# GpSimd loads tokens behind the normalising, TensorE projects ahead of the first turn of a half, ScalarE squares ahead of copying that turn

## The chip, the cores and the metric

The kernel runs on one core of a Trainium2 chip. The metric is the device time of one execution in microseconds; before the change three runs gave a median of 3911.52 us. The engines have a queue each and meet only through semaphores: TensorE (PE), VectorE (DVE), ScalarE (ACT), GpSimd (POOL) and the queue that issues the DMAs (SP).

## What is computed

The input has 8 batches of 512 tokens of 128 features. A causal attention and a stack of six layers start from the normalised input, and both results are added to the input. The part that the change touches is the attention of a layer of the stack, with 16 heads of 64 and windows of 32 keys:

```python
for i in range(DEPTH):                                   # DEPTH = 6
    x = attn_layer(shift_tokens(x), Wqkv[i], q_scale[i], k_scale[i], Wo[i]) + x
    x = ffn_layer(shift_tokens(x), ln_g[i], ln_b[i], W1[i], b1[i], W2[i], b2[i]) + x

def attn_layer(x, Wqkv, qs, ksc, Wo):
    q, k, v = heads(x @ Wqkv)
    q = l2norm(q) * qs; k = l2norm(k) * ksc
    q = q * cos * scale + rotate_half(q) * sin * scale
    k = k * cos * inv + rotate_half(k) * sin * inv
    out = local_attention(q, k, v)                       # each query sees its window and the one before
    return out.transpose(0, 2, 1, 3).reshape(b, n, INNER) @ Wo
```

## The kernel before

All tokens of the stack stay in SBUF, transposed (xT). After the causal attention (about the first 490 us of the span) a loop runs over the six layers. In a layer the attention goes over 32 tiles of 128 tokens, tile by tile, and the feed-forward part follows.

**The pipeline.** Every engine runs the same function `pipeline(eng, step)`: one step a tile, six steps written out, a loop of six passes over four steps, and eight steps written out, which end with the draining. `behind(t, i, part, lag)` gives the tile that is `lag` steps back. In one step the engines work on several tiles: tile n is projected, n-1 is turned (transposed), n-2 is scored, n-3 is exponentiated, normalised and turned, n-3 or n-4 is weighed, n-5 or n-6 is projected out.

**The halves of a step.** A step has two halves, `wp` 0 and 1. The queries and keys of a tile come in four chunks of 512 columns (0 and 1 are the queries, 2 and 3 the keys); half `wp` handles chunks 2wp and 2wp+1. A chunk goes through these stations:

- `project(c)` on PE: three matmuls into bank pj[c % 2] (operands split in a high and a low part, one matmul short of all four). It waits for `sq` and `rotd`, that is, until the chunk two back has been squared and rotated. project(0) waits for `xs_ready` too, which GpSimd's `rests_of_tile` gives.
- `square(c)` on ACT (line 940), from the bank; then `rotate(c)` on DVE (line 1236), which waits for the square (`sq`) and for the `add` of the chunk two back (two buffers t12).
- `add(c)` on POOL (line 1505), which waits for `rotd` and for the turn of the same chunk of the tile before (`tr`).
- `scale(lag, c)` on POOL (line 1519), with `rn`, the inverse norms that ACT's `norms` makes (lines 949 to 956): chunks 0 and 1 in half 1 of the same step, chunks 2 and 3 in half 0 of the next.
- `turn_qk(c)` on PE (line 614): four transposes into rbank, when the chunk is scaled (`qn`) and when the chunk before it has been copied out of rbank (`ev`).
- `turned_qk(c)` on ACT (line 790): copies rbank out, in two copies for chunks 0 and 1, in one for 2 and 3.

Beside these run: `score(wp)` on PE with the mask that ACT's `mask_ahead` puts into the bank beforehand (it waits for `sub`, the subtraction of the maximum on DVE, line 1259); `exp` on ACT; `sums` on DVE; `normalise` on POOL (line 1527); `turn_p` on PE (line 645), which waits for the normalised half (`pn`); `windows()` on PE (line 673, in half 1), which transposes the tile's tokens into rbank and waits until chunk 2 has been copied out of it; `weigh` and `project_out`.

**Loading tokens.** POOL's `load_tile` copies the shifted tokens of the tile two ahead into `xs` in two instructions (lines 1475 and 1477), each of which waits for POOL's own one before it; before the change it runs in half 1 between add(2) and the scaling, and waits until add(2) has ended (`add`). ACT's `heads_of_tokens` and POOL's `rests_of_tile` (line 1484) split them.

The halves of the three engines before the change, in the order of their queues:

```
PE    turn_qk(2wp), project(2wp), project(2wp+1), turn_p, [windows], weigh, score, turn_qk(2wp+1), project_out
ACT   mask_ahead, turned_qk(2wp), square(2wp), square(2wp+1), exp, norms, [windows], turned_p, weighed, [heads], turned_qk(2wp+1)
POOL  add(2wp), [load_next], scale, scale, normalise, add(2wp+1), [rests_of_tile]
```

DVE's half is rotate(2wp), rotate(2wp+1), sums, the maximum and its subtraction, the sums of squares, and in half 0 of every other step the update of xT.

Of the kernel before, what the change touches and what calls it, by code (L numbers as in the profile page):

```python
# [92 lines left out]
def build(nc, ins, out, layers=DEPTH):  # L93
    ctx = ExitStack()
    with ctx:
# [55 lines left out]
        qn = take(4, 512)  # L151
# [97 lines left out]
        def behind(t, i, part, lag):  # L249

            s = t - lag
            if (part == 0 and s < 0) or (part == 2 and s >= 2 * TT):
                return None
            return s % TT, i + s // TT
# [144 lines left out]
        def _(pe):  # L399
# [153 lines left out]
            with pe.Fori(0, layers) as l:  # L553
# [14 lines left out]
                def step(t, i, part):  # L568
# [33 lines left out]
                    def turn_qk(c):  # L602
                        if not (v := behind(t, i, part, 1)):
                            return
                        tt, bt = v
                        g = g_of(bt) * 16 + (4 * tt + c)
                        pe.wait_ge(S["qn"], g + 7)

                        if c == 3:
                            pe.wait_ge(S["xwev"], g_of(bt) * 4 + tt + 1)  # L610
                        else:
                            pe.wait_ge(S["ev"], g)
                        for j in range(4):
                            m = nc.tensor.transpose(rbank[:, j * P:(j + 1) * P], qn[:, c, j * P:(j + 1) * P],  # L614
                                                    ident[:, :])
                        m.then_inc(S["tr"], 1)
# [77 lines left out]
                    if part == 2 and t == LAG + 2 * TT - 1:  # L694
# [5 lines left out]
                        for b in range(4):  # L700
                            mean(b)
                    for wp in range(2):
                        turn_qk(2 * wp)
                        project(2 * wp)
                        project(2 * wp + 1)
                        turn_p(wp)
                        if wp == 1:
                            windows()
                        weigh(4 - wp, 1 - wp)
                        score(wp)  # L710
                        turn_qk(2 * wp + 1)
                        project_out(wp)
# [75 lines left out]
        def _(act):  # L788
# [121 lines left out]
            with act.Fori(0, layers) as l:  # L910
# [11 lines left out]
                def step(t, i, part):  # L922
# [98 lines left out]

                    for wp in range(2):
                        mask_ahead(3 - wp, 1 - wp)
                        turned_qk(2 * wp)
                        square(2 * wp)
                        square(2 * wp + 1)
                        exp(3 - wp, 1 - wp)
                        norms(1 - wp, 1 - wp)
                        if wp == 1:
                            windows()  # L1030
                        turned_p(wp)
                        weighed(4 - wp, 1 - wp)
                        if wp == 0 and not (part == 0 and t == 0) and (v := behind(t, i, part, -1)):
                            heads_of_tokens(*v)
                        turned_qk(2 * wp + 1)
# [364 lines left out]
        def _(pool):  # L1400
# [63 lines left out]
            with pool.Fori(0, layers) as l:  # L1464
                def load_tile(tt, bt, again):

                    g = (l * B + bt) * 4 + tt
                    if again:
                        pool.wait_ge(S["proj"], g * 4 - 12)
                        pool.wait_ge(S["xwt"], g - 2)  # L1470
                    c0, base = WIN + tt * P, bt * T + tt * P
                    late = 1 if tt == 0 else 0
                    lower, upper = xs[0:64, c0:c0 + P], xs[64:128, c0 + late:c0 + P]
                    x_lower, x_upper = xT[0:64, bass.ds(base, P)], xT[64:128, bass.ds(base - 1 + late, P - late)]
                    pt_(lower, x_lower, xs[0:64, 0:1].to_broadcast([64, P]), ALU.subtract).then_inc(S["xs_lower"], 1)  # L1475
                    pool.wait_ge(S["xs_lower"], g + 1)
                    pt_(upper, x_upper, xs[64:128, 0:1].to_broadcast([64, P - late]), ALU.subtract).then_inc(S["xs_part"], 1)  # L1477
                    pool.wait_ge(S["xs_part"], g + 1)

                def rests_of_tile(tt, bt):  # L1480
                    g = (l * B + bt) * 4 + tt
                    c0 = WIN + tt * P
                    pool.wait_ge(S["xs_high"], g + 1)
                    pt_(xs_lo[:, tt, :], xs[:, c0:c0 + P], xs_hi[:, tt, :].bitcast(F32), ALU.subtract)\  # L1484
                        .then_inc(S["xs_ready"], 1)

                def step(t, i, part):
                    def g_of(bt):
                        return l * B + bt

                    def load_next():
                        if v := behind(t, i, part, -2):
                            tt, bt = v
                            pool.wait_ge(S["add"], (g_of(bt) * 4 + tt) * 4 - 4)
                            load_tile(*v, not (part == 0 and t + 2 < TT))

                    def add(c):
                        if not (v := behind(t, i, part, 0)):
                            return
                        tt, bt = v  # L1500
                        g = g_of(bt) * 16 + (4 * tt + c)
                        pool.wait_ge(S["tr"], g)
                        pool.wait_ge(S["rotd"], g + 2)
                        swapped = t12[:, c % 2, 1, :].rearrange("p (h e d) -> p h e d", h=8, e=2)[:, :, ::-1, :]
                        pt_(qn[:, c, :].rearrange("p (h e d) -> p h e d", h=8, e=2),  # L1505
                            t12[:, c % 2, 0, :].rearrange("p (h e d) -> p h e d", h=8, e=2), swapped, ALU.add)\
                            .then_inc(S["add"], 1)

                    def scale(lag, c):
                        if not (v := behind(t, i, part, lag)):  # L1510
                            return
                        tt, bt = v
                        g = g_of(bt) * 16 + (4 * tt + c)
                        half = c // 2
                        pool.wait_ge(S["rn"], g_of(bt) * 8 + (2 * tt + half + 1))
                        pool.wait_ge(S["add"], g + 2)
                        r = rn[:, tt % 2, half, 8 * (c % 2):8 * (c % 2) + 8].unsqueeze(2).to_broadcast([P, 8, D])
                        sums_of_heads = qn[:, c, :].rearrange("p (h d) -> p h d", h=8)
                        pt_(sums_of_heads, sums_of_heads, r, ALU.mult).then_inc(S["qn"], 1)  # L1519

                    def normalise(lag, wp):
                        if not (v := behind(t, i, part, lag)):
                            return
                        tt, bt = v
                        m_ = g_of(bt) * 8 + 2 * tt + wp
                        pool.wait_ge(S["srec"], m_ + 1)
                        pt_(dd[:, wp, :].rearrange("p (h k) -> p h k", h=HP),  # L1527
                            dd[:, wp, :].rearrange("p (h k) -> p h k", h=HP),
                            srec[:, wp, :].unsqueeze(2).to_broadcast([P, HP, 64]), ALU.mult).then_inc(S["pn"], 1)

                    for wp in range(2):
                        add(2 * wp)
                        if wp == 1:
                            load_next()
                        scale(1 - wp, 2 - 2 * wp)
                        scale(1 - wp, 3 - 2 * wp)
                        normalise(3 - wp, 1 - wp)
                        add(2 * wp + 1)
                        if wp == 0 and not (part == 0 and t == 0) and (v := behind(t, i, part, -1)):
                            rests_of_tile(*v)  # L1540

                pool.wait_ge(S["mx"], l * B)
                pool.wait_ge(S["kT_zero"], 1)
                pool.wait_ge(S["ul"], l * (3 * B))
                load_tile(0, 0, False)
                rests_of_tile(0, 0)
                load_tile(1, 0, False)
                rests_of_tile(1, 0)
                pipeline(pool, step)

                with pool.Fori(0, B // 2) as j:
                    for e in range(2):
                        n = l * B + 2 * j + e
                        for c, (f0, fn) in enumerate(FCH):
                            pool.wait_ge(S["uh"], n * 3 + c + 1)
                            pt_(uu_lo[e][c][0:fn], uu[0:fn, e, c, :], uu_hi[e][c][0:fn].bitcast(F32), ALU.subtract)\
                                .then_inc(S["ul"], 1)
# [47 lines left out]
```

## Time and profile before

| | |
|---|---|
| median of 3 runs | 3911.52 us (3907.31 to 3912.17) |
| the profiled execution: its own time, its span | 3916.98 us, 3915.2 us |
| PE busy (matmuls) | 3617.0 us, 92% |
| PE busy (weight loads) | 2685.2 us, 69% |
| ACT busy | 3010.4 us, 77% |
| DVE busy | 2778.3 us, 71% |
| POOL busy | 2730.6 us, 70% |
| granted TensorE clock, mean | 0.96 |
| DMA | 5.8% of 16 engines' span |

Busy times are unions of an engine's instructions. Matmuls are pipelined and their ends are modelled, so that one matmul's row reaches into the next one's; what a matmul occupies is read from the distance between starts. In a row of the order in time, the time in brackets is how long the engine had been idle and who ended it; gaps under 0.15 us are not shown there and have to be read from the starts.

### The profile page before, as it was taken

To read this page: it belongs to the slowest core of one execution; us is meant where nothing else is said; L and a number is where in the kernel's file an instruction comes from. 1 tells how busy PE (TensorE), PEld (TensorE's weight loads), DVE (VectorE), ACT (ScalarE), POOL (GpSimd) and SP (SyncE) were. 2 spreads that over 40 slices of the span, in tenths; PEclk is the share of its full clock that TensorE was granted. 3 is DMA by queue.
4 is the path that set the end of the run, shared out by engine and by line. 5 is a ranking of instruction groups with operands and counts; after the bars stand their busy time and mean duration, and the time that the engine had idled before them with its cause. 6 is when DMAs were issued, how large, how long until landed. Compare 5 with 4: busy or idle time off the path is not lost.

```text
span 3915.2 us, 94663 instructions
## 1 busy us (share of the span) xinstructions
PE 3617.0 (92%) x30894; PEld 2685.2 (69%) x30894; DVE 2778.3 (71%) x3770; ACT 3010.4 (77%) x6096; POOL 2730.6 (70%) x2889
## 2 busy tenths in 40 slices
PE   6898689999889999899999899999799999799998
PEld 3444367777667777677777677777577776577776
DVE  4566377776677776677776677776677776677776
ACT  3555478888688887688887688886688886788885
POOL 3454378886388884588884688883688882788872
PEclk7999789999999999899999899999899999899999
DMA  4223200000100000000001000001000001000002
GB/s 132 85 90 92 56 1 1 0 0 1 30 2 1 0 0 22 9 2 0 0 0 29 2 2 0 0 0 29 2 2 0 0 0 29 2 1 0 0 1 71
DMA packets 59745, 67.76 MB, mean 17 GB/s; under 512 B 12006, under 2 KB 40164, under 8 KB 58468
## 3 DMA queue, kind: packets, MB, share of 16 engines
q1 hardware_dynamic: 59492, 64.64, 5.8%
q8 instruction: 128, 2.10, 0.2%
q14 instruction: 125, 1.02, 0.1%
HBM read 46.27 MB, written 18.35 MB: 17 GB/s over the span
## 4 chain that ended last, share of the span: by engine, by line
POOL 41%; issue 29%; PE 19%; ACT 5%; DVE 3%; POOLq 2%; DMA 1%; SPq 1%; ACTq 0%; DVEq 0%
PE bank L401 16%; POOL sb_area L1505 16%; POOL sb_area L1519 12%; POOL sb_area L1527 6%; POOL sb_xs L1477 2%; POOL sb_xs L1475 2%; POOL sb_xwin L1484 2%; PE bank L614 2%; ACT sb_area L790 1%; DVE sb_area L1157 1%; ACT sb_area L940 1%; ACT sb_area L983 1%; DMA sb_wqk_lo<-qk_rows 1%; ACT sb_area L842 0%; ACT sb_lnb L952 0%
## 5 line engine op out<-in xcount | busy, mean ns | idle before, releaser
L790 ACT ACTIVATE sb_area<-bank 128x512 f32<-128x512 f32 (+4 forms) x2149 | 1315.2, 648 | 266.2 <-PE bank L614 206.4
L1236 DVE TENSOR_TENSOR sb_area<-bank,sb_rots 128x1024 f32<-128x1024 f32 x768 | 907.4, 1220 | 625.6 <-ACT sb_area L940 619.0
L1505 POOL TENSOR_TENSOR sb_area<-sb_area 128x512 f32<-128x512 f32 x768 | 983.6, 1281 | 311.8 <-DVE sb_area L1236 311.3
L401 PE MATMUL bank<-sb_area 128*64 128x64 f32 (+6 forms) x17104 | 1053.9, 276 | 10.2 <-DMA sb_area<-in_c_crot 3.5
L401 PEld LDWEIGHTS bank<-sb_area 128*64 128x64 f32 (+4 forms) x17104 | 750.0, 146 | 280.8 <-issue 244.0
L1519 POOL TENSOR_TENSOR sb_area<-sb_area,sb_rn 128x512 f32<-128x512 f32 x768 | 785.0, 1043 | 49.9 <-POOL sb_xs L1477 40.8
L401 PE MATMUL bank<-sb_area,sb_wvo 128*128 128x256 f32 x3072 | 728.3, 381 | 3.1 <-DVE sb_xT L1291 3.1
L401 PE MATMUL bank<-sb_wqk_hi,sb_xwin 128*128 128x512 f32 x1536 | 606.6, 436 | 43.0 <-POOL sb_xwin L1484 38.4
L614 PE MATMUL bank<-sb_ident,sb_area 128*128 128x128 f32 x3072 | 507.3, 288 | 134.1 <-POOL sb_area L1519 90.0
L401 PEld LDWEIGHTS bank<-sb_area,sb_wvo 128*128 128x128 f32 x3072 | 555.0, 190 | 75.2 <-issue 8.8
L614 PEld LDWEIGHTS bank<-sb_ident,sb_area 128*128 128x128 f32 x3072 | 330.9, 143 | 304.4 <-POOL sb_area L1519 211.7
L940 ACT ACTIVATE sb_area<-bank 128x512 f32<-128x512 f32 x768 | 439.2, 597 | 82.8 <-PE bank L401 42.7
L1246 DVE TENSOR_REDUCE sb_ssq<-sb_area 128x16 f32<-128x1024 f32 x384 | 464.1, 1209 | 0.0
L1527 POOL TENSOR_TENSOR sb_area<-sb_area,sb_srec 128x512 f32<-128x512 f32 x384 | 401.2, 1045 | 81.1 <-DVE sb_srec L1271 81.1
L401 PE MATMUL bank<-sb_wqk_lo,sb_xwin 128*128 128x512 f32 (+4 forms) x1280 | 423.0, 414 | 29.7 <-POOL sb_xwin L1412 13.8
L401 PEld LDWEIGHTS bank<-sb_wqk_hi,sb_xwin 128*128 128x128 f32 x1536 | 303.3, 197 | 109.0 <-issue 43.4
L790 ACT ACTIVATE bank<-sb_lmask 128x512 f32<-128x512 bf16 x384 | 231.0, 601 | 100.7 <-DVE sb_area L1259 95.1
L1269 DVE TENSOR_REDUCE sb_ssum<-sb_area 128x8 f32<-128x512 f32 x384 | 260.0, 677 | 45.6 <-ACT sb_area L983 45.6
L1259 DVE TENSOR_TENSOR sb_area<-bank,sb_smax 128x512 f32<-128x512 f32 x384 | 265.6, 692 | 13.1
L1256 DVE TENSOR_REDUCE sb_smax<-bank 128x8 f32<-128x512 f32 x384 | 253.0, 659 | 24.8 <-PE bank L401 24.5
L401 PEld LDWEIGHTS bank<-sb_wqk_lo,sb_xwin 128*128 128x128 f32 (+1 forms) x1280 | 206.4, 200 | 88.5 <-issue 26.8
L1157 DVE TENSOR_REDUCE sb_area<-bank 128x2 f32<-128x1024 f32 (+3 forms) x256 | 203.6, 823 | 88.6 <-PE bank L401 87.1
(116 smaller groups left out, 4107.3 us busy)
## 6 DMA issues: line engine op xcount, KB each, us to landing
qk_rows<-sb_p SPq DMA_DIRECT2D x52, 256.0 KB, 4.2
sb_wqk_hi<-qk_rows SPq DMA_DIRECT2D x32, 256.0 KB, 2.9
sb_wqk_lo<-qk_rows SPq DMA_DIRECT2D x32, 256.0 KB, 2.7
sb_area<-in_Wqkv SPq DMA_DIRECT2D x7, 1024.0 KB, 5.7
sb_area<-in_WvT SPq DMA_DIRECT2D x7, 512.0 KB, 7.5
sb_wo_bd<-in_Wo SPq DMA_DIRECT2D x14, 256.0 KB, 8.5
sb_area<-in_x SPq DMA_DIRECT2D x4, 512.0 KB, 6.0
sb_area<-in_x SPq DMA_DIRECT2D x8, 256.0 KB, 2.9
```

The costliest lines, as they stand in the source:

```text
L401: return nc.tensor.matmul(o, a, b, start=start, stop=stop, skip_group_check=True)
L614: m = nc.tensor.transpose(rbank[:, j * P:(j + 1) * P], qn[:, c, j * P:(j + 1) * P], ident[:, :])
L790: return nc.scalar.activation(o, i, ACT.Copy)
L940: nc.scalar.activation(sqb[:, c, :], pj[c % 2][:, :], ACT.Square).then_inc(S["sq"], 1)
L1236: tt_(t12[:, c % 2, :, :].rearrange("p u (h d) -> p u h d", h=8), src, bc(rots[:, tt, s, :, :], [P, 2, 8, D], 2), ALU.mult).then_inc(S["ro ...
L1246: nc.vector.tensor_reduce(ssq[:, tt % 2, half, :], sqb[:, 2 * half:2 * half + 2, :].rearrange("p c (h d) -> p (c h) d", h=8), AX.X, ALU.add)\
L1256: nc.vector.tensor_reduce(smax[:, wp, :], s3, AX.X, ALU.max).then_inc(S["smax"], 1)
L1259: tt_(dd[:, wp, :].rearrange("p (h k) -> p h k", h=HP), s3, bc(smax[:, wp, :], [P, HP, 64], 2), ALU.subtract).then_inc(S["sub"], 1)
L1269: nc.vector.tensor_reduce(ssum[:, wp, :], d3, AX.X, ALU.add).then_inc(S["ssum"], 1)
L1505: pt_(qn[:, c, :].rearrange("p (h e d) -> p h e d", h=8, e=2), t12[:, c % 2, 0, :].rearrange("p (h e d) -> p h e d", h=8, e=2), swapped, A ...
L1519: pt_(sums_of_heads, sums_of_heads, r, ALU.mult).then_inc(S["qn"], 1)
L1527: pt_(dd[:, wp, :].rearrange("p (h k) -> p h k", h=HP), dd[:, wp, :].rearrange("p (h k) -> p h k", h=HP), srec[:, wp, :].unsqueeze(2).to_b ...
```

## The change

Three edits of the order within a half.

- PE: `project(2wp)` comes before `turn_qk(2wp)` instead of behind it; `project(2wp+1)` still follows.
- ACT: `square(2wp)` comes before `turned_qk(2wp)`.
- POOL: `load_next()` stands behind `normalise` and ahead of `add(2wp+1)` in half 1. Its wait for add(2) is replaced by waits for the scaling of chunks 0 and 1 of this tile and for the normalising just before it.

```diff
@@ PE
                     for wp in range(2):
+                        project(2 * wp)
                         turn_qk(2 * wp)
-                        project(2 * wp)
                         project(2 * wp + 1)
@@ ACT
                         mask_ahead(3 - wp, 1 - wp)
+                        square(2 * wp)
                         turned_qk(2 * wp)
-                        square(2 * wp)
                         square(2 * wp + 1)
@@ POOL
                         if v := behind(t, i, part, -2):
                             tt, bt = v
-                            pool.wait_ge(S["add"], (g_of(bt) * 4 + tt) * 4 - 4)
+                            pool.wait_ge(S["qn"], (g_of(bt) * 4 + tt) * 4)
+                            if last := behind(t, i, part, 2):
+                                pool.wait_ge(S["pn"], g_of(last[1]) * 8 + 2 * last[0] + 2)
                             load_tile(*v, not (part == 0 and t + 2 < TT))
@@
                         add(2 * wp)
-                        if wp == 1:
-                            load_next()
                         scale(1 - wp, 2 - 2 * wp)
                         scale(1 - wp, 3 - 2 * wp)
                         normalise(3 - wp, 1 - wp)
+                        if wp == 1:
+                            load_next()
                         add(2 * wp + 1)
```

## Rows read from the trace of the kernel before

**Rows 1.** The page's chain of work that ended last, by engine.

```profile
POOL 41%; issue 29%; PE 19%; ACT 5%; DVE 3%; POOLq 2%; DMA 1%; SPq 1%; ACTq 0%; DVEq 0%
```

**Rows 2.** Busy time by stretch: engines, then granted clock, DMA share, GB/s.

```profile
1632.00:1700.00 68.00, 52.43 (x430) 39.68 (x430) 47.91 (x53) 49.51 (x109) 54.91 (x58) 0.84 0.00 1
1700.00:2060.00 360.00, 353.84 (x3312) 274.36 (x3310) 279.56 (x362) 314.48 (x647) 306.37 (x325) 1.00 0.00 0
```

**Rows 3.** POOL in order of time: first add of a layer's first and last tile.

```profile
1632.05 2.65 POOL L1505 TENSOR_TENSOR sb_area<-sb_area 128x512 f32<-128x512 f32 x2 [2.17 <-DVE sb_area L1236]
...
2074.62 1.28 POOL L1505 TENSOR_TENSOR sb_area<-sb_area 128x512 f32<-128x512 f32 x1 [1.95 <-DVE sb_area L1236]
```

**Rows 4.** PE in order of time, one tile: half 1 from 2020.42, half 0 from 2027.63.

```profile
2020.42 0.63 PE L614 MATMUL bank<-sb_ident,sb_area 128*128 128x128 f32 x4
2020.81 0.48 PE L401 MATMUL bank<-sb_wqk_hi,sb_xwin 128*128 128x512 f32 x1
2021.13 0.40 PE L401 MATMUL bank<-sb_wqk_lo,sb_xwin 128*128 128x512 f32 x1
...
2022.30 0.60 PE L645 MATMUL bank<-sb_ident,sb_area 128*128 128x128 f32 x4
2022.73 0.38 PE L673 MATMUL bank<-sb_ident,sb_xs 128*128 128x128 f32 x2
2023.05 2.22 PE L401 MATMUL bank<-sb_area 64*128 64x256 f32 x40
...
2025.69 1.89 PE L401 MATMUL bank<-sb_area,sb_wvo 128*128 128x256 f32 x8
2027.63 0.66 PE L614 MATMUL bank<-sb_ident,sb_area 128*128 128x128 f32 x4
...
2029.63 0.66 PE L645 MATMUL bank<-sb_ident,sb_area 128*128 128x128 f32 x4
2030.22 2.22 PE L401 MATMUL bank<-sb_area 64*128 64x256 f32 x40
...
2032.86 1.89 PE L401 MATMUL bank<-sb_area,sb_wvo 128*128 128x256 f32 x8
2034.81 0.63 PE L614 MATMUL bank<-sb_ident,sb_area 128*128 128x128 f32 x4
```

**Rows 5.** POOL in order of time, from add(2) to the next tile's add(0).

```profile
2023.73 1.28 POOL L1505 TENSOR_TENSOR sb_area<-sb_area 128x512 f32<-128x512 f32 x1 [0.69 <-DVE sb_area L1236]
2025.34 0.39 POOL L1475 TENSOR_TENSOR sb_xs<-sb_xT,sb_xs 64x128 f32<-64x128 f32 x1 [0.33 <-POOL sb_area L1505]
...
2026.53 2.04 POOL L1519 TENSOR_TENSOR sb_area<-sb_area,sb_rn 128x512 f32<-128x512 f32 x2 [0.23 <-POOL sb_xs L1477]
2028.54 1.04 POOL L1527 TENSOR_TENSOR sb_area<-sb_area,sb_srec 128x512 f32<-128x512 f32 x1
...
2031.48 1.27 POOL L1505 TENSOR_TENSOR sb_area<-sb_area 128x512 f32<-128x512 f32 x1 [0.67 <-DVE sb_area L1236]
```

**Rows 6.** ACT in order of time, half 0.

```profile
2028.32 1.20 ACT L790 ACTIVATE sb_area<-bank 64x512 f32<-64x512 f32 x2 [0.79 <-PE bank L614]
2029.55 1.08 ACT L940 ACTIVATE sb_area<-bank 128x512 f32<-128x512 f32 x2
...
2031.71 0.22 ACT L956 ACTIVATE sb_rn<-sb_lnb 128x16 f32<-128x16 f32 x1
...
2033.48 1.18 ACT L790 ACTIVATE sb_area<-bank 64x512 f32<-64x512 f32 x2
2034.68 0.60 ACT L790 ACTIVATE bank<-sb_lmask 128x512 f32<-128x512 bf16 x1
```

**Rows 7.** DVE in order of time, half 0: the two rotations, the subtraction.

```profile
2030.18 2.36 DVE L1236 TENSOR_TENSOR sb_area<-bank,sb_rots 128x1024 f32<-128x1024 f32 x2 [2.16 <-ACT sb_area L940]
...
2033.95 0.69 DVE L1259 TENSOR_TENSOR sb_area<-bank,sb_smax 128x512 f32<-128x512 f32 x1
```

**Rows 8.** PE in order of time, turn of the second tile of a layer.

```profile
1639.25 0.80 PE L614 MATMUL bank<-sb_ident,sb_area 128*128 128x128 f32 x4 [2.66 <-POOL sb_area L1519]
```

## The prediction

> **What bounds the kernel now.** I looked first at how the time is shared between stages. From the first add of a layer's first tile to the first add of its last one 2074.62 - 1632.05 = 442.6 us pass [rows 3], six times over; the rest of a layer (the draining, the feed-forward part) and the causal part ahead of the layers hold none of the edited steps' steady running. I then read the busy time by stretch [rows 2]. In the 360 us in the middle of a layer the granted clock is 1.00, the upper level of 2.4 GHz, and PE is busy for 353.84 us, while ACT, POOL and DVE have 314, 306 and 280. In the first 68 us of a layer PE has only 52.43 and the clock is 0.84: there PE waits.
>
> That row says "PE is full", the chain of what ended last says "POOL 41%, PE 19%" [rows 1]. The order in time settles it, because a matmul's row reaches into the next one's. I compare equal steps of PE in the two halves of one tile [rows 4]:
>
> - The eight matmuls of `project_out` show 1.89 us, of which 0.38 is the last one's own length; seven starts in 1.51 make 0.216 each, 1.73 for eight. The next turn starts 1.94 us (2025.69 to 2027.63) and 1.95 us (2032.86 to 2034.81) after the first of them. So PE stands idle for 0.21 and 0.22 us ahead of each `turn_qk(2wp)`.
> - Turn and projections take 1.88 us in half 1 (2020.42 to 2022.30) and 2.00 in half 0 (2027.63 to 2029.63): 0.12 idle ahead of turn_p(0).
> - turn_p and the hand-over to weighing take 0.59 in half 0 (2029.63 to 2030.22). In half 1 the four transposes take 0.43, and the windows' two, which end with the same hand-over, take 0.32 where two alone would take 0.22: 0.43 + 0.10 = 0.53. That is 0.06 more.
>
> Together 0.61 us of a tile's 14.39 (2020.42 to 2034.81); PE's own work is 13.78 us a tile. Who ends these waits: the scaling of chunk 0 ends at about 2027.57, halfway in a row of two that starts at 2026.53, and turn_qk(0) starts at 2027.63; the normalising ends at 2029.58, and turn_p(0) starts at 2029.63 [rows 4, 5]. Before turn_qk(2) it is ACT's copy of chunk 1, which ends at 2034.66 [rows 4, 6].
>
> So one round closes a tile, and it goes through all engines: normalise, turn_p(0), weigh, score, turn_qk(1), project_out, turn_qk(2), its copy, square(2), rotate(2), add(2), **the load**, the two scalings, normalise. The load stands in it with 2026.53 - 2023.73 = 2.80 less an add of 1.28, 1.52 us [rows 5]. A second round through turn_qk(0), its two copies, square(0) and rotate(0) explains why add(0) waits for 0.67 us [rows 5 to 7].
>
> **The change, part by part.** I lay the new order out from the start of project(0), call that moment 0, and look for what is late next.
>
> *GpSimd.* Nothing is added but a wait. add(2) to the end of add(3) held 7.09 us of unbroken work (2023.73 to 2030.82: the normalising starts at 2028.54 and takes 1.00 to the next start, the add 1.28) [rows 5], and still does, since the load only changes its place. Scalings and normalising come 1.52 us earlier. The two waits of PE on them were 0.21 and about 0.18 us long, so both vanish, with over 1.1 us to spare. The load now waits for the normalising instead of for add(2): the same kind of wait for its own engine, 0.33 before the first and 0.23 behind the second instruction [rows 5], cost 0. What is behind it in the queue is add(3), at the same distance from add(2) as before.
>
> *TensorE.* project(0) no longer stands behind turn_qk, and waits for squares and rotations two chunks back, which are over half a step old. turn_qk(2wp) comes 0.79 later: the copy of chunk 1, 0.19 late before, is now in time. The price: six projection matmuls in one go take 1.49 us (2020.81 to 2022.30), the first 0.32 (to 2021.13), so the others 0.234 each [rows 4]. Now each group of three may begin with a slow start: at most 0.32 - 0.23 = 0.09 a half, 0.18 a tile; at least 0, since the trace has no projection directly behind a project_out. I take the middle, 0.09: PE's work is 13.87, between 13.78 and 13.96.
>
> *ScalarE.* The first chunk is ready 0.32 + 0.23 + 0.40 + about 0.04 = 0.99 after its projection starts. In the old half 0, ACT runs without a visible gap from 2028.32 to 2035.28 (the mask's 2034.68 + 0.60), 6.96 us [rows 6]; the new order holds the same pieces. So square(2) starts at 7.95, ends at 8.55 (two squares in 1.08, one some 0.60), and the copy of chunk 2 (about 0.61) ends at 9.16. PE waits for that copy before `windows`: project(0) to project(2) takes 6.83 (old half 0 is 7.18, less the waits of 0.22, 0.12 and 0.06, plus half of the 0.09 for this half; at most 0.05 more), then 1.94 for the two projections around the turn and 0.43 for turn_p: 9.20. With a crossing of 0.04 to 0.15 (2034.66 to 2034.81 is 0.15) PE waits for 0 to 0.11 there. I add 0.03. DVE's rotate(2) follows square(2) at once, before the copy, which is what the edit is for.
>
> A tile then takes **13.90 us instead of 14.39, 0.49 less**, between 13.78 and 14.07.
>
> *How many tiles.* 26 of the 31 distances in a layer at 14.39 make 374 us, and leave 68 for the five of the filling, 13.7 each. So 6 x 26 = 156 tiles gain 0.49: 76 us. In the filling PE waits much longer, 2.66 us in one place, for the same scaling [rows 8], and its busy time is 52 of 68 us [rows 2]: there the round is the bound, and the edits take from it the load (1.52) and the copies ahead of the squares (1.20 and 0.60). Part of this runs into PE's own work and into the half-speed clock, so I bound it by 0 and 2 us a tile and take 1: 6 x 5 x 1 = 30 us. The draining, I hold, is unchanged.
>
> **Sum.** 3917.0 us (the profiled execution's own time, span 3915.2) - 76 - 30 = 3811. The median of the runs shown, 3911.5, lies 5.5 lower, so I forecast 3806.
>
> **A rule against the row on busy time.** Read as it stands, the row of the middle stretch leaves 360 - 353.84, or 1.7%, 0.25 us a tile, to be gained at most [rows 2]; the starts leave 0.61. By the first the edits can bring 156 x 0.25 = 38 us and no more, 3874. The Trainium skill (Perfetto Trace Analysis, Identifying the Most-Contended Engine) says that the busy share of matmuls is no good measure of how near TensorE is to its limit, and wants the weight loads looked at. By that rule there is more room than 1.7%; the trace agrees in that weight loads are busy for 274.36 of the 360 us, 76%.
>
> **Rivals.**
>
> 1. *PE is as full as its busy time says.* For it: 98% busy, clock at its upper level. Against it: the unequal lengths of equal steps in [rows 4]. Time: 3874. Chance 0.07.
> 2. *ScalarE takes over the wait.* Its copy of chunk 2 is due within 0.1 us by my sum. If ACT's half gets 0.3 us longer (square and copy no longer overlap as two squares do, or the mask waits), PE waits for it at `windows`: 14.20 a tile, nothing in the filling; 156 x 0.19 = 30 us, 3882. For it: ACT has no gap in that half. Against: 0.6 us between the subtraction's end (2034.64) and the mask in the new order. Chance 0.06.
> 3. *Slower: the load in front of add(3).* add(3) frees the buffer that rotate(1) of the next tile writes. add(2) starts at 6.83 + 2.92 (0.99 + 0.60 + 0.03 + 1.22 + 0.08) = 9.75, and add(3) ends 7.09 later, at 16.84, which is 2.94 in the next tile. rotate(1) wants to start behind square(1), at 3.43, and the subtraction ends 3.3 after that start (2030.18 plus half of the pair's 2.36 is about 2031.3; 2033.95 + 0.69 is 2034.64 [rows 7]), at 6.75; the mask is due at 7.35. So there are 0.5 + 0.6 = 1.1 us of slack; beyond it each us of delay is one in the tile, through mask, square(2), rotate(2), add(2). It decides against the change when the load's way is more than 1.6 us longer than now, twice its length. With 2.1 us, 14.90 a tile: 156 x 0.51 = 80 us more, 3991. For it: GpSimd has 7.09 us of work in a half of 7.04. Against: nothing in the load changes. Chance 0.07.
> 4. *No change.* Another round of 14.39 us stands behind the one removed, one that I have not seen. The distances above show none. 3911. Chance 0.05.
>
> **How the numbers follow.** My forecast has 0.75. Its own range is 156 x (0.32 to 0.61) = 50 to 95 us and 0 to 60 in the filling: 3756 to 3862. About 2% of a tile either way covers the rest; reaching to the first rival's time, without rivals 2 to 4, gives 3755 to 3875, which leaves out about 0.2. Changes under 0.2% (8 us) cannot be told from none here. Faster: 0.75 + 0.07 + 0.06 = 0.88; same 0.05; slower 0.07.
>
> **What would show it.** In the changed profile, starts of turn_qk(0) one tile apart are 13.9 us apart (13.8 to 14.05). No idle time in brackets before L614 by POOL L1519 in the middle of a layer; if one is left on PE it is before L673, by ACT L790. The load's 0.33 follows L1527. POOL's wait for DVE before add(0) is gone or shorter, and a wait of some 0.5 us for ACT's L956 appears before the scaling in half 0, since rn, 3.61 after the first copy's start [rows 6], is ready at 4.6 and add(0) is over at 4.2; it costs nothing, as turn_qk(2) is due at 7.6. The first five tiles of a layer take 62 to 64 us instead of 68. I am wrong if a tile stays over 14.1, if the idle time of PE moves to L673 with more than 0.15 us, or if the matmuls behind project_out start at more than 0.32.

## The result: 3754.85 us, 4% less

The changed kernel takes 3754.85 us (median of 4 runs, 3744.81 to 3760.0) where the kernel before takes 3911.85 in the same comparison. The ratio is 0.9596, with a 95% interval of 0.9572 to 0.962: 157 us less. The forecast was 3806, with a range from 3755 to 3875. The direction was right, and so was the round of waits that the change was to open. But the gain was half as large again as predicted (157 us for 105), one of the three edits was credited with what the other two do, and the time lies 0.15 us outside the range.

The profiled execution took 3744.81 us, its span is 3743.1. Its chain of work that ended last, by engine, answers to [rows 1]:

```profile
PE 75%; issue 11%; ACT 5%; DVE 3%; POOL 3%; DMA 1%; SPq 1%; ACTq 0%; POOLq 0%; DVEq 0%
```

It was POOL with 41% and is PE with 75%. The busy time by stretch of the third layer, its filling and its middle (the columns are those of [rows 2]):

```profile
1568.80:1632.00 63.20, 50.37 (x442) 37.78 (x443) 51.16 (x58) 51.53 (x114) 58.19 (x62) 0.91 0.01 1
1632.00:1980.00 348.00, 347.95 (x3408) 285.58 (x3407) 290.93 (x370) 313.54 (x661) 312.18 (x330) 1.00 0.00 0
```

In the middle the busy rows of PE leave no idle time, and its weight loads are busy for 82% (76% before). In the filling the granted clock is 0.91 where it was 0.84. The first add of that layer's first and last tile, in GpSimd's order of time, answers to [rows 3]:

```profile
1568.81 2.65 POOL L1507 TENSOR_TENSOR sb_area<-sb_area 128x512 f32<-128x512 f32 x2 [2.16 <-DVE sb_area L1236]
...
1983.57 1.28 POOL L1507 TENSOR_TENSOR sb_area<-sb_area 128x512 f32<-128x512 f32 x1 [1.25 <-DVE sb_area L1236]
```

That is 414.8 us instead of 442.6. PE's order of time for one tile, half 1 from 1863.79 and half 0 from 1870.81, with the project_out ahead of it, answers to [rows 4]:

```profile
1862.25 1.89 PE L401 MATMUL bank<-sb_area,sb_wvo 128*128 128x256 f32 x8
1863.79 0.58 PE L401 MATMUL bank<-sb_wqk_hi,sb_xwin 128*128 128x512 f32 x1
1864.20 0.40 PE L401 MATMUL bank<-sb_wqk_lo,sb_xwin 128*128 128x512 f32 x1
...
1864.67 0.65 PE L614 MATMUL bank<-sb_ident,sb_area 128*128 128x128 f32 x4
1865.08 0.48 PE L401 MATMUL bank<-sb_wqk_hi,sb_xwin 128*128 128x512 f32 x1
...
1865.87 0.60 PE L645 MATMUL bank<-sb_ident,sb_area 128*128 128x128 f32 x4
1866.31 0.39 PE L673 MATMUL bank<-sb_ident,sb_xs 128*128 128x128 f32 x2
...
1869.27 1.89 PE L401 MATMUL bank<-sb_area,sb_wvo 128*128 128x256 f32 x8
1870.81 0.59 PE L401 MATMUL bank<-sb_wqk_hi,sb_xwin 128*128 128x512 f32 x1
...
1871.71 0.60 PE L614 MATMUL bank<-sb_ident,sb_area 128*128 128x128 f32 x4
1872.06 0.48 PE L401 MATMUL bank<-sb_wqk_hi,sb_xwin 128*128 128x512 f32 x1
...
1872.84 0.60 PE L645 MATMUL bank<-sb_ident,sb_area 128*128 128x128 f32 x4
...
1877.55 0.58 PE L401 MATMUL bank<-sb_wqk_hi,sb_xwin 128*128 128x512 f32 x1
```

No row has a bracket. A tile is 13.76 us long here (1863.79 to 1877.55) and 13.69 as a median. From the first matmul of project_out to turn_p it is 3.57 us in half 0 (1869.27 to 1872.84), and 3.62 in this half 1 (1862.25 to 1865.87), where the turn takes 0.41 us to the next start instead of 0.35. The parts of the kernel before were 1.73 + 1.88 = 3.61 by the prediction's reading, and its turn in there took 0.39 (2020.42 to 2020.81); with a turn of 0.35 they are 3.57 too. So the new order costs PE nothing.

GpSimd from add(2) to the next add(0), as in [rows 5], but in the new order:

```profile
1908.05 1.28 POOL L1507 TENSOR_TENSOR sb_area<-sb_area 128x512 f32<-128x512 f32 x1 [0.39 <-DVE sb_area L1236]
1909.28 2.05 POOL L1521 TENSOR_TENSOR sb_area<-sb_area,sb_rn 128x512 f32<-128x512 f32 x2
1911.28 1.05 POOL L1529 TENSOR_TENSOR sb_area<-sb_area,sb_srec 128x512 f32<-128x512 f32 x1
1912.71 0.39 POOL L1475 TENSOR_TENSOR sb_xs<-sb_xT,sb_xs 64x128 f32<-64x128 f32 x1 [0.38 <-POOL sb_area L1529]
1913.29 0.40 POOL L1477 TENSOR_TENSOR sb_xs<-sb_xT,sb_xs 64x128 f32<-64x128 f32 x1 [0.18 <-POOL sb_xs L1475]
1913.85 2.52 POOL L1507 TENSOR_TENSOR sb_area<-sb_area 128x512 f32<-128x512 f32 x2 [0.17 <-POOL sb_xs L1477]
```

The last row holds add(3) and add(0) back to back: between add(2) and the next tile's add(0) GpSimd waits for no other engine any more, only for its own instructions. One half earlier it waits for the norms, here 0.28 us (0.45 in the next tile):

```profile
1902.95 2.04 POOL L1521 TENSOR_TENSOR sb_area<-sb_area,sb_rn 128x512 f32<-128x512 f32 x2 [0.28 <-ACT sb_rn L956]
```

To compare kernels below I use one figure, worked out from each trace in the same way: the distance between the first rotations (line 1236) of neighbouring tiles, as the median over the 7th to 30th distance of all six layers ("a tile"), and the sum of a layer's first five distances, averaged over the layers ("the filling"). Before: 14.38 and 67.4 us. After: 13.69 and 58.3 us.

### The profile page after: what moved, and what is told of

Same layout as the page of the kernel before. It is cut to its first block, busy times and chain, and to the rows that moved or that the text cites. A ratio compares the mean times of both kernels' runs of the same rounds, so it can differ in the third digit from the quotient of the medians.

```text
span 3743.1 us, 94975 instructions
## 1 busy us (share of the span) xinstructions
PE 3498.2 (93%) x30894; PEld 2693.9 (72%) x30894; DVE 2811.2 (75%) x3770; ACT 2958.4 (79%) x6096; POOL 2729.9 (73%) x2889
## 4 chain that ended last, share of the span: by engine, by line
PE 75%; issue 11%; ACT 5%; DVE 3%; POOL 3%; DMA 1%; SPq 1%; ACTq 0%; POOLq 0%; DVEq 0%
PE bank L401 60%; PE bank L614 10%; PE bank L645 4%; ACT sb_area L790 2%; PE bank L673 1%; DVE sb_area L1157 1%; POOL sb_area L1521 1%; DMA sb_wqk_lo<-qk_rows 1%; ACT sb_area L940 1%; ACT sb_area L842 0%; ACT sb_area L983 0%; POOL sb_area L1507 0%; ACT sb_wqk_hi L790 0%; DVE sb_smax L1256 0%; DVE sb_area L1259 0%
## 5 line engine op out<-in xcount | busy, mean ns | idle before, releaser
L1236 DVE TENSOR_TENSOR sb_area<-bank,sb_rots 128x1024 f32<-128x1024 f32 x768 | 923.9, 1222 | 424.2 <-ACT sb_area L940 395.1
L401 PE MATMUL bank<-sb_wqk_hi,sb_xwin 128*128 128x512 f32 x1536 | 725.1, 474 | 43.2 <-POOL sb_xwin L1484 38.6
L940 ACT ACTIVATE sb_area<-bank 128x512 f32<-128x512 f32 x768 | 459.1, 598 | 190.2 <-PE bank L401 179.8
L614 PE MATMUL bank<-sb_ident,sb_area 128*128 128x128 f32 x3072 | 490.9, 283 | 74.1 <-ACT sb_area L790 57.3
L614 PEld LDWEIGHTS bank<-sb_ident,sb_area 128*128 128x128 f32 x3072 | 344.9, 142 | 180.9 <-POOL sb_area L1521 75.1
L401 PE MATMUL bank<-sb_wqk_lo,sb_xwin 128*128 128x512 f32 (+4 forms) x1280 | 414.3, 404 | 29.1 <-POOL sb_xwin L1412 13.6
L1259 DVE TENSOR_TENSOR sb_area<-bank,sb_smax 128x512 f32<-128x512 f32 x384 | 265.5, 691 | 13.1
```

The lines of the kernel that those rows point to most:

```text
L401: return nc.tensor.matmul(o, a, b, start=start, stop=stop, skip_group_check=True)
L940: nc.scalar.activation(sqb[:, c, :], pj[c % 2][:, :], ACT.Square).then_inc(S["sq"], 1)
L1236: tt_(t12[:, c % 2, :, :].rearrange("p u (h d) -> p u h d", h=8), src, bc(rots[:, tt, s, :, :], [P, 2, 8, D], 2), ALU.mult).then_inc(S["ro ...
L1259: tt_(dd[:, wp, :].rearrange("p (h k) -> p h k", h=HP), s3, bc(smax[:, wp, :], [P, HP, 64], 2), ALU.subtract).then_inc(S["sub"], 1)
```

## The experiments

All ran three rounds against the kernel before, whose medians were 3913.6, 3913.5 and 3904.5 in the three groups (e1 to e4, e5 to e8, e9 to e11).

**The three edits one by one and in pairs (e1 to e4, e9, e10).** The edits are those of the diff ahead; each kernel has some of them.

e1, TensorE's alone:

```diff
+                        project(2 * wp)
                         turn_qk(2 * wp)
-                        project(2 * wp)
```

> TensorE's edit alone (project(2wp) ahead of turn_qk(2wp)), ScalarE and GpSimd as before. Theory (the round through all engines sets the pace, and it goes through ScalarE's order): ScalarE still copies the first turn before it squares, so square(2wp) now waits for a turn that comes 0.79 us later; the round gets longer by about 0.35 us a tile. A tile takes 14.6 to 14.8 us instead of 14.4: 30 to 50 us slower than before, about 3950. Rival (each edit brings a share of the gain by itself): faster than before by a third of the gain, about 3860. Rival 2 (GpSimd's load is what mattered): same as before.

Measured 3934.73 us, ratio 1.005 (1.0033 to 1.0067); a tile 14.62.

e2, ScalarE's alone:

```diff
+                        square(2 * wp)
                         turned_qk(2 * wp)
-                        square(2 * wp)
```

> ScalarE's edit alone (square(2wp) ahead of the copy of the first turn), TensorE and GpSimd as before. Theory: TensorE turns first and projects then, so the finished turn waits on ScalarE for a square whose projection is 0.7 us behind it, and the copies end about 0.7 us later; the next turns wait for them. A tile takes 15.0 to 15.2 us: 100 to 120 us slower, about 4030. Rival (rotate gets its square earlier and that is what sets the pace): faster than before, about 3860.

Measured 4036.16 us, ratio 1.032 (1.0302 to 1.0337); a tile 15.08.

e3, GpSimd's alone (load_next behind normalise, with its new waits):

> GpSimd's edit alone (the load behind the normalising). Theory: the load's 1.52 us leave the round through normalise and turn_p(0), but the turn, its copy and the square stay in line, and the waits move to that round: a tile takes about 14.2 us instead of 14.4, and the filling gets some us shorter. 35 to 60 us faster than before, about 3865. Rival (the load was the whole matter): all of the 157 us.

Measured 3847.08 us, ratio 0.9833 (0.9816 to 0.9849); a tile 14.11.

e4, TensorE's and ScalarE's, without GpSimd's:

> Both edits of TensorE and ScalarE, GpSimd's load left between add(2) and the scaling. Theory: with the projection ahead, the scaling is needed 2 us later, so that the load's 1.52 us are covered where they stand; TensorE stays without a wait in the middle of a layer, 13.7 us a tile, and the only loss is in the filling: within 25 us of the changed kernel, about 3765. Rival (the load was part of what set the pace): TensorE waits for line 1519 again in the middle of a layer, 13.9 to 14.2 a tile, 3800 or more.

Measured 3760.14 us, ratio 0.9606 (0.9583 to 0.9628); a tile 13.79.

e9, TensorE's and GpSimd's:

> The edits of TensorE and GpSimd, ScalarE as before (it copies the first turn, then squares). Theory (the copy ahead of the square is a link of the round that is left): with the scaling early, the round is turn, copies, square, rotate, add, scale; a tile takes about 14.2 to 14.3 us, 3850 to 3870. Rival (GpSimd's and TensorE's edits are enough): 13.7 a tile, 3755.

Measured 3829.03 us, ratio 0.9809 (0.9789 to 0.9829); a tile 14.12.

e10, ScalarE's and GpSimd's:

> The edits of ScalarE and GpSimd, TensorE as before (it turns first, then projects). Theory: the loss of ScalarE's edit alone (15.1 us a tile) comes from the turn's copy waiting for the square and from the next turn waiting for the copy, which has nothing to do with the load: GpSimd's edit brings nothing here, 15.0 to 15.2 a tile, about 4030, the filling a little shorter. Rival (the load's 1.52 us come off every tile): 14.0 to 14.4, 3850 to 3900.

Measured 3998.07 us, ratio 1.024 (1.0219 to 1.026); a tile 15.05.

Together, with a tile and the filling worked out as above:

```
edits                       a tile   filling   ratio to before
none                        14.38    67.4      1
GpSimd                      14.11    65.1      0.9833
TensorE                     14.62    66.8      1.005
ScalarE                     15.08    67.5      1.032
TensorE, GpSimd             14.12    62.5      0.9809
ScalarE, GpSimd             15.05    63.7      1.024
TensorE, ScalarE            13.79    57.4      0.9606
all three                   13.69    58.3      0.9596
```

Nothing here adds up. TensorE's and ScalarE's edits cost 0.5% and 3.2% each by itself and bring 3.9% together: either engine's new order is right only when the other has it too. GpSimd's brings 1.7% alone and nothing that the intervals can tell once the other two are in.

Four of the six expectations missed in size. e1 lost 21 us, not 30 to 50. e3 gained 67 us, a little over the 35 to 60. e9 gained 76 us and came to 3829, ahead of the 3850 to 3870. In e10 GpSimd's edit was to bring nothing, and it brought 0.8% (1.024 against e2's 1.032), most of it in the filling, 63.7 against 67.5 us. e2 and e4 came out as expected in time.

One idle row of PE for each of the first three shows the link that is left. Each is from PE's order of time in the middle of a layer; first e1, in front of turn_p:

```profile
1938.32 0.66 PE L645 MATMUL bank<-sb_ident,sb_area 128*128 128x128 f32 x4 [0.64 <-POOL sb_area L1527]
```

PE waits there for the normalising, as it did before the change, only longer. In e2 it waits for ScalarE's copy, and ScalarE (second fence) for the projection behind the turn:

```profile
1937.62 0.66 PE L614 MATMUL bank<-sb_ident,sb_area 128*128 128x128 f32 x4 [0.75 <-ACT sb_area L790]
```

```profile
1931.14 0.60 ACT L940 ACTIVATE sb_area<-bank 128x512 f32<-128x512 f32 x1 [1.56 <-PE bank L401]
1931.64 1.18 ACT L790 ACTIVATE sb_area<-bank 64x512 f32<-64x512 f32 x2
```

The turn is ready, but its copy stands behind the square in ScalarE's queue. In e3 turn_qk(0) no longer waits for its scaling: it starts 1.73 us after project_out, which is project_out's own length. What is left stands before turn_qk(2), which starts 2.10 us after project_out (1929.75 to 1931.85) where it was 1.95:

```profile
1929.75 1.89 PE L401 MATMUL bank<-sb_area,sb_wvo 128*128 128x256 f32 x8
1931.85 0.63 PE L614 MATMUL bank<-sb_ident,sb_area 128*128 128x128 f32 x4 [0.21 <-POOL sb_area L1521]
...
1937.11 1.89 PE L401 MATMUL bank<-sb_area,sb_wvo 128*128 128x256 f32 x8
1938.84 0.60 PE L614 MATMUL bank<-sb_ident,sb_area 128*128 128x128 f32 x4
```

The bracket names GpSimd's scaling, but that turn needs chunk 2 only, the first of the two in GpSimd's row, which was scaled at about 1930.8. What ended just before it is ScalarE's copy of chunk 1, at 1931.71:

```profile
1929.76 2.05 POOL L1521 TENSOR_TENSOR sb_area<-sb_area,sb_rn 128x512 f32<-128x512 f32 x2
```

```profile
1930.53 1.18 ACT L790 ACTIVATE sb_area<-bank 64x512 f32<-64x512 f32 x2
```

So with the load out of the way PE waits for the copies: turn, copy and square are still in line.

In e4 the load stands where it stood, and the chunk-0 scaling is done at about 1921.6, 0.9 us ahead of turn_qk(0) at 1922.53. Only turn_p(0) is still held in some tiles, here by 0.15 us: it starts 0.38 after the last projection instead of 0.23, behind the normalising, which ends at 1923.68.

```profile
1920.63 2.05 POOL L1519 TENSOR_TENSOR sb_area<-sb_area,sb_rn 128x512 f32<-128x512 f32 x2 [0.23 <-POOL sb_xs L1477]
1922.63 1.05 POOL L1527 TENSOR_TENSOR sb_area<-sb_area,sb_srec 128x512 f32<-128x512 f32 x1
```

```profile
1922.53 0.60 PE L614 MATMUL bank<-sb_ident,sb_area 128*128 128x128 f32 x4
...
1923.43 0.40 PE L401 MATMUL bank<-sb_wqk_hi,sb_xwin 128*128 128x512 f32 x1
1923.81 0.65 PE L645 MATMUL bank<-sb_ident,sb_area 128*128 128x128 f32 x4
```

**Who sets the pace: TensorE's work cut by 0.86 us (e5, e6).** Both kernels leave out 4 of the 8 matmuls of project_out in half 1, so their output lacks a share of the heads.

```diff
-                            for h in range(4 * k, 4 * k + 4):
+                            for h in range(4 * k, 4 * k + (2 if k in (0, 2) else 4)):
```

e5, on the kernel before:

> The kernel before, with 4 of the 8 matmuls of project_out left out in half 1 (two heads of four of the parts 0 and 2; the output lacks these heads' share). Four matmuls are 0.86 us of TensorE's work a tile. Theory (before the change TensorE does not set the pace): behind these matmuls TensorE waits for GpSimd's scaling anyway, so a tile stays at 14.4 us and the idle time before turn_qk(0) grows from 0.2 to 1.1; the time is that of before, within 10 us (a little less in the last steps of a layer). Rival (TensorE at 98% busy is the bound): 0.8 us less a tile, 130 us faster.

Measured 3886.26 us, ratio 0.9927 (0.9904 to 0.9949). A tile stays at 14.39, and PE's idle time grows from 0.21 by the 0.86:

```profile
1934.84 1.03 PE L401 MATMUL bank<-sb_area,sb_wvo 128*128 128x256 f32 x4
1936.93 0.65 PE L614 MATMUL bank<-sb_ident,sb_area 128*128 128x128 f32 x4 [1.06 <-POOL sb_area L1519]
```

The bound of 10 us was missed: it is 27 us faster. Most of them come from the draining, which I had not costed: from the first rotation of a layer's last tile to that of the next layer 122.6 us pass instead of 126.6, six times 4. So in these last steps PE's own work counted before the change too.

e6, on the changed kernel:

> The changed kernel with the same 4 matmuls left out in half 1 (the output lacks these heads' share). Theory (now TensorE's own work is the pace): a tile takes less by up to 0.86 us, until the next engine sets the pace; GpSimd's work of about 13.1 us a tile with its waits for ScalarE's norms comes next, so 13.0 to 13.3 instead of 13.7: 70 to 110 us below the changed kernel, about 3660. Rival (a round through several engines still sets the pace): a tile stays at 13.7.

Measured 3634.52 us, ratio to before 0.9283 (0.926 to 0.9305), 120 us below the changed kernel; a tile 13.11. The time was expected at 70 to 110 us below; the rest is the draining again, 123.1 us instead of 127.1, six times. The tile gives up 0.58 of the 0.86 us, and then GpSimd is full but for short waits for DVE ahead of add(2): none in this tile, 0.20 and 0.24 us in its neighbours. (The 0.16 us of the first row stand behind line 1477 like the 0.17 of the last, which is GpSimd's wait for itself.)

```profile
1900.69 2.52 POOL L1507 TENSOR_TENSOR sb_area<-sb_area 128x512 f32<-128x512 f32 x2 [0.16 <-DVE sb_area L1236]
1903.16 2.05 POOL L1521 TENSOR_TENSOR sb_area<-sb_area,sb_rn 128x512 f32<-128x512 f32 x2
1905.17 1.05 POOL L1529 TENSOR_TENSOR sb_area<-sb_area,sb_srec 128x512 f32<-128x512 f32 x1
1906.17 1.29 POOL L1507 TENSOR_TENSOR sb_area<-sb_area 128x512 f32<-128x512 f32 x1
1907.41 0.46 POOL L1484 TENSOR_TENSOR sb_xwin<-sb_xs,sb_xwin 128x128 fp32r<-128x128 f32 x1
1907.93 1.28 POOL L1507 TENSOR_TENSOR sb_area<-sb_area 128x512 f32<-128x512 f32 x1
...
1913.74 2.52 POOL L1507 TENSOR_TENSOR sb_area<-sb_area 128x512 f32<-128x512 f32 x2 [0.17 <-POOL sb_xs L1477]
```

The same cut brings a tile nothing before and 0.58 after. TensorE's own work was not the pace, and now is.

**How much room GpSimd has: one more instruction of 1.0 us behind the load (e7, e8).**

```diff
+        idle = sb("idle", [512])
...
                             load_tile(*v, not (part == 0 and t + 2 < TT))
+                            pt_(idle[:, :].rearrange("p (a b) -> p a b", a=4), ident[:, :].unsqueeze(1).to_broadcast([P, 4, P]), ident[:, :].unsqueeze(1).to_broadcast([P, 4, P]), ALU.add)
```

e7, on the changed kernel:

> The changed kernel with one more GpSimd instruction of about 1.0 us (an addition of a constant to itself into a tile nobody reads) right behind the load, ahead of add(3). It measures how much room GpSimd has in its half. Prediction's rival 3 had 1.1 us of slack behind add(3): then a tile stays at 13.7 to 13.8, no change. Theory now: GpSimd's own 13.1 us and its wait for the norms leave about 0.5 us; with 1.0 more GpSimd sets the pace: 14.1 to 14.3 a tile, 70 to 100 us slower than the changed kernel.

Measured 3821.82 us, ratio to before 0.9771 (0.9747 to 0.9796), 67 us above the changed kernel; a tile 14.02. Behind the load, in GpSimd's order of time:

```profile
1936.41 0.40 POOL L1478 TENSOR_TENSOR sb_xs<-sb_xT,sb_xs 64x128 f32<-64x128 f32 x1 [0.18 <-POOL sb_xs L1476]
1936.89 1.04 POOL L1499 TENSOR_TENSOR sb_idle<-sb_ident 128x512 f32<-128x512 f32 x1
1937.89 2.52 POOL L1509 TENSOR_TENSOR sb_area<-sb_area 128x512 f32<-128x512 f32 x2
```

From the second instruction of the load to add(3) it is 1.48 us (1936.41 to 1937.89), where the changed kernel has 0.56 from the same place (1913.29 to 1913.85): the instruction lengthens GpSimd's way by 0.92. And VectorE's rotate(1) now waits for add(3):

```profile
1939.27 1.23 DVE L1237 TENSOR_TENSOR sb_area<-bank,sb_rots 128x1024 f32<-128x1024 f32 x1 [1.40 <-POOL sb_area L1509]
```

e8, on the kernel before:

> The kernel before with the same GpSimd instruction of about 1.0 us behind the load, where the load stands before: between add(2) and the scaling. Theory (the load is a link of the round that sets the pace): the whole 1.0 us is added to every tile, 15.4 instead of 14.4, some 170 us slower than before. Rival (TensorE or ScalarE sets the pace, GpSimd is 70% busy): under 50 us slower.

Measured 4062.07 us, ratio 1.0382 (1.0359 to 1.0405): 148 us more; a tile 15.24, 0.86 more. PE's wait for the scaling grows with it:

```profile
1943.08 0.65 PE L615 MATMUL bank<-sb_ident,sb_area 128*128 128x128 f32 x4 [0.99 <-POOL sb_area L1521]
```

Before, the instruction costs 0.86 us in every tile, though GpSimd is 70% busy: it is a link. (It takes the place of part of the gap behind line 1477, which is why it is not 1.0.) After the change it costs 0.33 of its 0.92: GpSimd has 13.69 - 13.11 = 0.6 us of room, and what goes beyond it is paid. Both losses are under what was expected (70 to 100 and 170 us), which had counted the instruction in full.

**One step further (e11).** Both projections ahead of the first turn, both squares ahead of its copy:

```diff
                         project(2 * wp)
-                        turn_qk(2 * wp)
                         project(2 * wp + 1)
+                        turn_qk(2 * wp)
...
                         square(2 * wp)
-                        turned_qk(2 * wp)
                         square(2 * wp + 1)
+                        turned_qk(2 * wp)
```

> A step further in the same direction: TensorE does both projections of a half ahead of the first turn, ScalarE both squares ahead of its copy; GpSimd as changed. If the gain grew with how far the projections are ahead, this would be as fast or faster, 3740 to 3755, and the filling shorter. Theory: the first turn's copy now ends about 1.2 us later in ScalarE's half, and TensorE, which needs the bank of that copy for its second turn and the copy of chunk 2 for its windows, waits there: 14.3 to 14.5 a tile, 3860 to 3880.

Measured 3869.95 us, ratio 0.9915 (0.9894 to 0.9936), 115 us above the changed kernel; a tile 14.43. In the middle of a layer PE waits where it was expected to, ahead of `windows`, for the copy of chunk 2:

```profile
1935.06 0.44 PE L673 MATMUL bank<-sb_ident,sb_xs 128*128 128x128 f32 x2 [0.49 <-ACT sb_area L790]
```

One projection ahead is enough to cover the turn's wait; the second only delays a copy that somebody needs. No kernel that does the whole work was faster than the changed one.

## Why the prediction was right in kind and too small in size

What failed are the two terms of the sum that make the gain: 156 tiles at 0.49 us, 76 us, measured 110; and the filling at 1 us a tile, 30 us, measured 55. Beside them the prediction credited GpSimd's edit with waits that the other two edits remove. That the time misses the range by only 0.15 us says nothing for the range: the forecast itself was off by 51 us.

**Where the time came from.** From a layer's first tile to its last the changed kernel needs 27.4 us less (443.0 to 415.6, mean of six layers, by first rotations): 164 us. 9.1 of the 27.4 lie in the filling, 18.3 in the other 26 distances. The stretches between layers are 0.1 to 0.7 us longer. The profiled execution also started its layers 11 us earlier, in a part that no edit touches; that is scatter, and the medians differ by 157.

**Right: what closed the tile.** The prediction's round of normalise, turns, copies, squares, rotations, adds and load was the pace. e5 shows that PE's own work was not, e8 that the load was a link, e1 to e3 that each engine's order is another. Rival 1 (PE as full as its busy time says, 3874) fell: PE was 98% busy and a tile gave up 0.69 us. The Trainium skill (Perfetto Trace Analysis, Identifying the Most-Contended Engine) calls the busy share of matmuls a poor measure of the distance to TensorE's limit and asks for the weight loads' share. The outcome agrees: weight loads went from 76% to 82% of the middle stretch at the same clock.

**Right: what came next.** PE's idle time is gone, and its own work is the bound (e6). Rival 2 (ScalarE takes over at `windows`) did not occur in the changed kernel, but e11 shows that it lies close: there PE stands idle for 0.49 us at that place. Of the signs named in advance these came: no wait before L614 is in the rows, none at line 673, add(0) no longer waits for DVE, the load's wait (0.38) follows the normalising (now line 1529), and a wait for the norms appears, 0.28 to 0.45 us instead of 0.5. Two were off: a tile is 13.69 us, below the 13.8 to 14.05, and the filling takes 58.3, not 62 to 64. And one sign of being wrong came: the projection behind project_out starts with 0.41, over the 0.32 named as the most. It did no harm, for the reason under (a).

**Mis-sized: a tile, 13.90 forecast, 13.69 measured.** Three small terms were wrong in one direction. (a) "Now each group of three may begin with a slow start", taken at 0.09: the projection's first start is slow (0.41, 1863.79 to 1864.20), but it comes 0.03 us behind the last start of project_out (7 x 0.216 = 1.51 after 1862.25 is 1863.76) instead of 0.216, and the two cancel: project_out, projections and turn take 3.57 us in either order, once the turn is counted at 0.35 in both. (b) 0.03 for waiting at `windows`: none. (c) The 13.78 for PE's own work was too high by 0.08. A turn that begins behind a wait is slower itself: 0.39 us to the next start (2020.42 to 2020.81) against 0.35 without a wait (1871.71 to 1872.06), 0.04 in each half, and the prediction's parts held the slower one. And (d), the gain was taken from 14.39, while one tile in four, where the loop goes round, took 14.72: the mean of the middle distances was 14.46 and is 13.72. So a tile gave 0.74 us there, not 0.49, and the 26 distances of a layer 18.3 us, not 12.7: 34 us more than forecast.

**Mis-sized: the filling, 1 us a tile forecast, 1.8 measured.** 67.4 to 58.3 is 9.1 us a layer, 55 in all, not 30: 25 us more. (34 and 25 are 59, where the medians miss the forecast by 51; 3 of the difference are the stretches between layers, the rest is within the scatter of the part ahead of them.) The bound of 2 us a tile held, the choice of its middle didn't. The experiments tell the edits apart there too: GpSimd's alone takes 2.3 us off the filling, TensorE's and ScalarE's together 10.0. The granted clock rose from 0.84 to 0.91 in that stretch with PE busier; how much of the 9.1 us is the clock and how much the shorter round was not separated.

**Wrong: GpSimd's share.** The prediction lets both waits vanish because scalings and normalising "come 1.52 us earlier". The load's move brings nothing that the times can tell on top of the others: 0.9606 without and 0.9596 with it. In the trace of e4 the first wait is gone without the move, and of the second 0.15 us is left in some tiles, 13.79 us a tile against 13.69. The reason is in the prediction's own layout. With add(2) at 9.75, the load where it stood would let the scaling of chunk 0 end at 9.75 + 2.80 + 1.04 = 13.6, and turn_qk(0) is due at 13.90 + 0.79 = 14.7: the two other orders alone give 1.1 us there (0.9 in e4), which covers the load. I had not asked what each edit brings given the others.

**Wrong: the slack of rival 3.** It gave GpSimd 1.1 us before a longer load would cost anything. e7 put 1.0 us there and it cost 0.33 a tile. The reckoning followed one buffer (add(3) to the next rotate(1)) and left out the plain sum of GpSimd's work over both halves, about 13.1 us, which leaves 0.6. The wait that it named does stand in e7, 1.40 us of rotate(1) behind add(3); how much of the 0.33 goes through it, and how much is GpSimd's sum, was not separated. The rival did not come about since nothing in the load became longer.

## What to carry to other kernels

When several engines pass work round in a ring, compare equal steps of the busiest one by the distance of their starts: 98% busy hid 0.6 us of waits in a tile of 14.4. Reorder the producer and the consumer together; one without the other was 0.5% and 3.2% slower here, the two together 3.9% faster. When a bracket names an engine, see in that engine's own rows whether it ended just then: in e3 it was another. And sum each engine's own work over the whole period before believing in slack along one path: it is the floor that comes next, here 13.7 us for TensorE and 13.1 for GpSimd.

## What the runs showed that was not expected

Changing from one kind of matmul to another cost TensorE nothing: the slow first start of a projection (0.41 us behind project_out, 0.32 behind transposes, 0.23 otherwise) is made up by its coming 0.03 us after the last start of the group before, whose own distance would be 0.216 or 0.11.

Every fourth tile is longer, and the loop has four steps in a pass: 14.72 against 14.38 us in the kernel before, 13.83 against 13.68 in the changed one. The other kernels in which PE waits for a ring of engines lie between 0.09 (e10) and 0.34 us, so who sets the pace does not settle that cost.

The part ahead of the layers, the same code in all kernels, is uneven from one execution to the next: the first rotation comes between 473.5 and 495.1 us in the profiles. A single profiled execution can be some 10 us off for that alone, so differences of that size were read from distances inside the layers.
